# A graph layer on one core: the gather of node rows goes to GpSimd alone, and the edge product takes two tiles at once

## What is computed

```python
msg  = relu(x[src] + edge_attr @ We + be)
aggr = segment_sum(msg, dst, num_segments=N)
h    = (1.0 + eps) * x + aggr
h    = relu(h @ W1 + b1) @ W2 + b2
h    = relu((h - mean(h)) * rsqrt(var(h) + 1e-5) * gamma + beta) + x      # over the nodes
out  = layernorm(x + h)                                                   # over the features
```

## Time and profile before

| | us |
|---|---|
| device time, median of 3 | 1582.13 |
| device time, lowest and highest | 1579.88, 1583.58 |
| span of the profiled execution | 2684.1 |
| that execution's own time | not given; the page has the span alone |
| PE busy in the span (23395 matmuls) | 1871.5 |
| POOL busy (1179 gathers among 1193 instructions) | 1154.5 |
| DVE busy | 991.5 |
| ACT busy | 841.5 |

### The profile page before, as it was taken

One profiled execution on the slowest core, in us unless ns is written; L12 is line 12 of the kernel. 1 busy time (PEld: TensorE's weight loads), 2 busy tenths in 40 slices (PEclk: granted clock), 3 DMA queues, 4 the chain that ended last, 5 costly groups with the idle time before them and its releaser, 6 DMA issues.

```text
span 2684.1 us, 58837 instructions
## 1 busy us (share of the span) xinstructions
PE 1871.5 (70%) x23395; PEld 1369.8 (51%) x23395; DVE 991.5 (37%) x3361; ACT 841.5 (31%) x1954; POOL 1154.5 (43%) x1193
## 2 busy tenths in 40 slices
PE   1776777776777777677767767767767776766776
PEld 0455555555555555555555555555555555555554
DVE  6433333333333333333333333333333333333335
ACT  3232323232332333232323323323223322322335
POOL 6444444444444444444444444434434444444421
PEclk9877788787887787788888778878778778887888
DMA  8222222232222222222222222222222222222221
GB/s 231 62 59 65 62 59 68 59 71 66 63 63 61 61 62 64 61 66 59 67 61 61 65 61 63 65 58 65 64 58 67 61 62 63 63 65 62 62 86 50
DMA packets 148455, 180.61 MB, mean 67 GB/s; under 512 B 41677, under 2 KB 128932, under 8 KB 147924
## 3 DMA queue, kind: packets, MB, share of 16 engines
q1 hardware_dynamic: 102489, 89.62, 14.0%
q0 software_dynamic: 37728, 77.31, 11.5%
q10 hardware_dynamic: 7963, 9.90, 1.2%
HBM read 170.09 MB, written 6.63 MB: 66 GB/s over the span
## 4 chain that ended last, share of the span: by engine, by line
PE 66%; issue 20%; another core or an unknown queue 8%; ACT 2%; DVE 1%; ACTq 0%; DVEq 0%
PE ps L1330 23%; PE ps L1315 15%; PE ps L1255 12%; PE ps L1269 11%; PE ps L1296 1%; PE ps L1276 1%; PE ps L1299 1%; ACT xg L694 1%; PE ps L1287 1%; PE ps L1384 1%; ACT slotS L680 0%; PE ps L1288 0%; PE ps L1394 0%; DVE lnst L1197 0%
## 5 line engine op out<-in xcount | busy, mean ns | idle before, releaser
L574 POOL DMA_INDIRECT xg<-xb,idxb x1145 | 1106.6, 966 | 1423.9 <-DVE msg L937 1068.8
L1330 PE MATMUL ps<-iota_all 128*128 128x128 bf16 x4032 | 377.8, 247 | 425.7 <-issue 291.3
L688 ACT ACTIVATE iota_all<-ps 128x384 bf16<-128x384 f32 x896 | 408.5, 489 | 775.6 <-remote 567.8
L1330 PEld LDWEIGHTS ps<-iota_all 128*128 128x128 bf16 x4032 | 290.1, 111 | 515.6 <-issue 511.5
L1022 DVE TENSOR_TENSOR accT<-accT,ps 128x64 f32 x390 | 86.5, 222 | 1138.4 <-remote 992.8
L1255 PE MATMUL ps<-we,ea 64*128 64x128 f32 x3126 | 344.2, 367 | 45.7 <-issue 45.3
L1330 PE MATMUL ps<-iota_all,hot_all 128*128 128x128 bf16 x4032 | 301.1, 229 | 102.6 <-issue 98.8
L937 DVE TENSOR_TENSOR msg<-ps,xg 128x512 f32<-128x512 f32 x390 | 262.0, 686 | 238.9 <-PE ps L1255 233.2
L1330 PEld LDWEIGHTS ps<-iota_all,hot_all 128*128 128x128 bf16 x4032 | 247.2, 102 | 172.4 <-issue 145.0
L1255 PEld LDWEIGHTS ps<-we,ea 64*128 64x128 f32 x3126 | 288.0, 261 | 80.7 <-issue 72.2
L1269 PE MATMUL ps<-msg,hot 128*64 128x128 f32 x3120 | 300.9, 352 | 6.2 <-issue 4.5
(11 more groups left out here) (135 smaller groups left out, 1113.8 us busy)
## 6 DMA issues: line engine op xcount, KB each, us to landing
ea<-in_eat SPq DMA_DIRECT2D x156, 320.0 KB
lowB<-lowD SPq DMA_DIRECT2D x128, 224.0 KB
xg<-xb,idxb POOLq DMA_INDIRECT x1145
accT<-in_xt ACTq DMA_DIRECT2D x1, 3125.0 KB
x<-in_xt ACTq DMA_DIRECT2D x1, 3125.0 KB
iota_all<-in_x ACTq DMA_DIRECT2D x1, 3080.0 KB
out<-iota_all SPq DMA_DIRECT2D x5, 512.0 KB
xb<-iota_all SPq DMA_DIRECT2D x3, 784.0 KB, 6.2
```

What stands on the lines that cost most here:

```text
L574: pool.indirect_dma_start(out=xg[0:rows, slot, j, :], out_offset=None, in_=of, in_offset=bass.IndirectOffsetOnAxis(ap=index, axis=0)).then ...
L688: act.activation(rows3[:, t, :, :].rearrange("p a h -> p (a h)"), ps_rows(k * NTILE + t), ACT.Copy)\
L1330: last = pe.matmul(found[:, e, :], sel2[set_of(k)][:, t, e * P:(e + 1) * P], rows3[:, t, a, :], start=(t == 0 and e == 0 and a == 0), stop ...
```

## The change

The new kernel has nothing of TensorE's share. `x3`, the sets, the sorting, the picks and the joins are gone, and with them the lists that SP sent to HBM and back. All 1563 tiles are gathered by GpSimd, one indirect DMA for each as before, and the ring still has 15 places. The indices of all groups come in three loads at the start rather than in 78 loads along the way.

`linear` takes two tiles at once. The weights are the 128 rows of `ea` (64 features of one tile above 64 of another), and the moving operand is `we2`, 256 columns with We on the diagonal blocks and zero elsewhere; one matmul gives two tiles side by side. `place(j)` puts a group's tiles in the matching order. `msg` and `hot` have four sets instead of three; the window sums, the turned sums and `winS` have two; the edge product has two banks for each half. VectorE writes the one-hot of a pair ahead of its additions and adds a window three pairs late (`LAG`). The turned `x` that the end needs has a place of its own (`xT`) and is loaded once. The early chunks start in the last 12 pairs, one a pair.

```diff
-    RING = ROUND // 2
-    TURN = 3
+    RING = 15
+    TURN = 4
+        def place(j):
+            return (0, 2, 1, 3)[j]
+        def ps_two(m, half, c):
+            return ps[:, m % 2 * 2 + half, 2 * c * HID:2 * (c + 1) * HID]
...
-                    for j in range(by_pool(i, g)):
-                        gather(g % RING, j, P, idxb[h][:, at + j:at + j + 1], s_xg[g % RING], xb if biased else x)
+                if g == UNBIASED:
+                    for q in range(NQ):
+                        pool.wait_ge(s_xb[q], stores(q))
+                if g >= RING:
+                    wait_apart(pool, s_pre, g - RING + 1)
+                for j in range(GROUP):
+                    gather(g % RING, place(j), P, idx_all[:, h, at + j:at + j + 1], s_xg[g % RING],
+                           x if g < UNBIASED else xb)
...
-            def linear(h, s, half, tiles):
-                for j, r in tiles:
-                    rows, at = slice(j // 2 * EDIM, (j // 2 + 1) * EDIM), j % 2 * P
-                    last = pe.matmul(ps_lin(half, j)[0:r, :], ea[h][rows, s, at:at + r], we2[rows, :], start=True, stop=True)
+            def linear(m, half):
+                h, s = divmod(2 * m + half, SPAN)
+                if s == 0:
+                    pe.wait_ge(s_ea[h % PARTS], (h // PARTS + 1) * 32)
+                for c in range(2):
+                    last = pe.matmul(ps_two(m, half, c), ea[h % PARTS][:, s, c * P:(c + 1) * P],
+                                     we2[:, :, :].rearrange("k c h -> k (c h)"), start=True, stop=True)
                 last.then_inc(s_lin, 1)
...
+            for p in range(PAIRS):
+                one_hot(p)
+                add_x(p, 0)
+                add_x(p, 1)
+                if p >= LAG:
+                    add_window(p - LAG)
...
+            for p in range(PAIRS):
+                if p >= 2:
+                    pe.wait_ge(s_pre, 2 * (p - 1))
+                for half in range(2):
+                    linear(p, half)
+                if p >= 2:
+                    window(p - 2)
+                if p >= LAG:
+                    turn(p - LAG)
```

More of the change, by code:

```diff
@@ L130, in gine_layer_kernel @@
     BY_ACT = 4
-    assert BATCHES[-1][0] + BATCHES[-1][1] == NBLK and N < FAR and NSUB * SUB - N < SUB
-    BANK = BANKW
+    assert BATCHES[-1][0] + BATCHES[-1][1] == NBLK
+    FLAGS = 8
+    LAG = 3
+    CLOSE = PAIRS - EARLY
+    DONE = [2 * (CLOSE + c - LAG) for c in range(EARLY)]
+    BANK = 512
     WALL = -(-N // BANK)
@@ L1258, in _ @@
-            ALL = [(j, P) for j in (0, 2, 1, 3)]
-            def window(q, pair):
-                pe.wait_ge(s_msg, 2 * pair + 2)
-                pe.wait_ge(s_hot, pair + 1)
-                if not isinstance(pair, int) or pair:
-                    pe.wait_ge(s_winS, pair)
-                    pe.wait_ge(s_acc, 2 * pair)
-                for j in range(GROUP):
-                    for half in range(2):
-                        last = pe.matmul(ps_win[half * WIN:(half + 1) * WIN, :], hot[:, q % TURN, half * GROUP + j, :],
-                                         msg[:, q % TURN, half * GROUP + j, :], start=(j == 0), stop=(j == GROUP - 1))
-                last.then_inc(s_win, 1)
@@ new lines, in linear_last @@
+            def linear_last(m):
+                h, s = divmod(2 * m, SPAN)
+                pe.wait_ge(s_ea[h % PARTS], (h // PARTS + 1) * 32)
+                for j, r in LAST:
+                    c, at = j // 2, j % 2 * P
+                    rows = slice(c * EDIM, (c + 1) * EDIM)
+                    last = pe.matmul(ps_lin(m, 0, j)[0:r, :], ea[h % PARTS][rows, s, at:at + r], we2[rows, c, :],
+                                     start=True, stop=True)
+                last.then_inc(s_lin, 1)
@@ new lines, in window @@
+            def window(m):
+                pe.wait_ge(s_msg, 2 * m + 2)
+                pe.wait_ge(s_hot, m + 1)
+                if m >= 2:
+                    pe.wait_ge(s_winS, m - 1)
+                    pe.wait_ge(s_acc, 2 * (m - 1))
+                if m < PAIRS:
+                    for j in range(GROUP):
+                        for half in range(2):
+                            last = pe.matmul(ps_win(m)[half * WIN:(half + 1) * WIN, :], hot[:, m % TURN, half * GROUP + j, :],
+                                             msg[:, m % TURN, half * GROUP + place(j), :],
+                                             start=(j == 0), stop=(j == GROUP - 1))
+                else:
+                    for j, r in LAST:
+                        last = pe.matmul(ps_win(m)[0:WIN, :], hot[0:r, m % TURN, j, :], msg[0:r, m % TURN, place(j), :],
+                                         start=(j == 0), stop=(j == LASTT))
+                last.then_inc(s_win, 1)
@@ L1410, in _ @@
-            run(pe, iteration)
-            general, redo = held
-            pe.wait_ge(s_ea[0], (ITERS * (SPANS // PARTS) + 1) * 32)
-            pe.wait_ge(s_pre, LASTG)
-            linear(0, 0, 0, LAST)
-            window(STEPS - 1, LOOPED // 2 - 1)
-            turn(LOOPED // 2 - 1)
-            pe.wait_ge(s_msg, LASTG + 2)
-            pe.wait_ge(s_hot, LASTG // 2 + 1)
-            for m, (j, r) in enumerate(LAST):
-                last = pe.matmul(ps_end, msg[0:r, LASTG // 2 % TURN, j, :], hot[0:r, LASTG // 2 % TURN, j, :],
-                                 start=(m == 0), stop=(m == len(LAST) - 1))
```

905 lines of the change are left out of this document (217 added, 688 removed).

## The result

The changed kernel takes **2062.39 us** (2057.66 to 2065.16), the kernel before 1582.34 us beside it. The ratio is 1.3026, with a 95% interval of 1.2998 to 1.3053: 30% slower, 24 us above the 2038 us of the forecast and inside its range of 1985 to 2100. The profiled execution took 2065.16 us, 2.2 us more than its span.

What follows compares the result with a forecast made beforehand. GpSimd's issue of gathers was taken as the bound. Start 3.5, gathers 1950.6, lifts 4.3, `xb` wait 2, one-hots 36 and end 41.2 sum to 2038 us, 29% slower; range 1985 to 2100 us.

Steps and rivals of the forecast that it cites:

- GpSimd is the bound before, and its step is 1.248 us: Kernel before: GpSimd issues gathers nearly without a pause, one every 1.248 us, 1179 of them making 1471.4 us.
- The term of 1950.6 us: Main loop after the change: 1563 gathers on GpSimd at 1.248 us each.
- The reason given for the long profile: Profile before: its 2684.1 us span against 1582 timed was taken as the price of recording TensorE's instructions.
- 57 us left, within 2 to 4% of the bound: Kernel before: steps and ends sum to 1525 us, leaving 57 of 1582, of which contention takes some 24.
- TensorE stays under GpSimd's 9.98 us a pair: New loop: TensorE needs 6.5 us a pair, with up to 4.2 for the edge product, against GpSimd's 9.98.
- The rival that TensorE binds at 2385 us: New loop: single matmuls really run one behind another, 11.8 us a pair, so TensorE sets the time; chance 3%.
- The shared wait at the start: Early part: gathers held under the four lifts lose 4.3 us, which stay after the change.
- The wait for `xb`: After the first 40 gathers: GpSimd's old wait of 8.7 us becomes 0 to 10 us, taken as 2.
- The one-hots, 36 us: Loop: one-hots falling at random meet a gather's start in 54% of pairs, holding it 0.34 us; 0 to 133 us.
- The rival that saw the tie and let every one-hot meet at the full 0.68 us (2135 us): Loop: one-hots follow landings at a fixed distance, so all meet gathers, costing 133 us; over 2100 us, chance 8%.
- The end, 41.2 us: Last gather to end: 37.0 us from the last product, plus landing, additions, clips, last window's 0.9; 39 to 54.
- Nothing for what lies around the span: Outside the profiled span: what a run has around it wasn't given, so nothing was added.

Runs made afterwards that it cites:

- e3_fewer: The changed kernel with 1188 of its 1563 gathers, some tiles in every third group from group 15 on left out: 1594.80 us.
- b_again: The kernel before, unchanged, run once more for a second profiled execution: 1586.59 us.
- e5_before_less: The kernel before with two of four gathers left out, from the second round on, in each group that is GpSimd's alone; TensorE's work unchanged: 1479.31 us.
- e1_iota_psum: The changed kernel with one operand of the one-hot moved from SBUF to PSUM, except in the last 12 pairs: 2014.88 us.
- e9_before_scalar: The kernel before with the one-hot of a pair made by eight scalar-compare instructions in place of one with two SBUF operands: 1569.43 us.

## Why the prediction was right, step by step

- **GpSimd is the bound before, and its step is 1.248 us.** Right. The step was read from a profile that showed another bottleneck, and it held: 1.248 before, 1.251 after, 1.247 by `e3_fewer`. The term of 1950.6 us came out at 1955.3.
- **The reason given for the long profile was wrong.** The earlier trace rows were read as the price of recording TensorE's instructions. `b_again` has all of them and spans 1584.5 us; `e5_before_less` has 58353 and spans 1477.7 us in an execution of 1479.52. The choice to lean on the distance between gathers was good, the reason for it wasn't: that the step held is in part luck, since nobody knew what had disturbed that execution. Another execution, not an argument, settled it.
- **"57 us left, within 2 to 4% of the bound".** Too cautious. In `b_again` the sum is 3.4 until the first gather, 1471.4 of steps, 7.6 for `xb`, 5.4 lost in the first 31 gathers (34.7 busy against 31 x 0.944), 45.9 in the 1145 behind them (1126.8 against 1145 x 0.944), and 47.2 from the last gather's end to the end: 1580.9 of 1584.5 us. The contention I had at 20 us was 45.9, and the end I had at 41 was 47.2.
- **TensorE stays under GpSimd's 9.98 us a pair.** Right. Two edge products took 2.24 and 3.43 us where up to 4.2 was allowed, and the longest of all 3.8; with 1.98 for the window and 0.48 for the turn the dearest pair has 6.2 us, where 6.5 was reckoned. The rival that TensorE binds at 2385 us is out.
- **The shared wait at the start.** 4.3 us kept, measured 4.0 (41.9 busy for 40 gathers against 40 x 0.947). The wait for `xb` was put at 2 us between 0 and 10, and was 3.9. The cause is the one that the prediction feared, the load of all indices ahead of the stores on SP's queue:

```profile
7.65 35.75 SPq L299 DMA_DIRECT2D idx_last<-in_src_col  x3
...
43.44 8.24 SPq L305 DMA_DIRECT2D xb<-iota_all  x4
```

  SP gets through these loads only at 43.4 us, and the first store of `xb` goes out at 43.44 us, though its lift was done at 32; in `b_again` it goes out at 36.94, as soon as its lift is done. The first gather from `xb` starts at 61.23 us and there at 54.92. The first gather of all started at 3.56 us, after 1.9 us of waiting for its own indices.
- **The one-hots, 36 us.** The right mechanism, mis-sized: 50.3 us, 0.26 us a pair where 0.185 was worked out. The step that failed is "if it falls at random". Starts spread evenly would meet 54% of the one-hots and be held for 0.34 us each. In the trace 151 of 190 are met, 79%, most of them within 0.25 us of their start, and 50.3/151 is 0.33 us each. VectorE's pair follows the landing of a gather, and the landing follows GpSimd's steps, which ties the one to the other. In 106 of 188 pairs the one-hot starts 3.5 to 3.8 us behind the start of the last gather of the pair before, and three steps are 3.75 us. The 0.34 us for each is right by luck. A gather that starts later than 0.03 us into the one-hot is held until 0.82 us behind its end (the 0.87 read from the earlier trace rows is 0.82 there too: 1016.21 less 1015.39). That is 0.13 us less than its own 0.947, so it loses 0.56 us less its start, and not what is left of the one-hot. Evenly spread starts would then cost some 0.11 us a pair, 22 us in all (an estimate from these rows); 36 was too much for the case described, and too little for the one that came. The rival that saw the tie and let every one-hot meet at the full 0.68 us (2135 us) had its reason right and its size too large: the truth lies between the two. This term is the larger half of the 24 us missing.
- **The end, 41.2 us.** Measured 45.3, from 2017.73 to 2063.0 us. The step that was too small is the 0.9 us for the last window's copy and turn. From the last group's product to the next product (W1), after the change and in `b_again`:

```profile
2022.45 1.70 PE L844 MATMUL ps<-msg,hot 128*64 128x128 f32 x6 [0.85 <-DVE accT L644]
...
2026.90 1.81 PE L857 MATMUL ps<-accT,w1s 128*128 128x220 f32 x4 [1.90 <-issue]
```

```profile
1547.43 1.15 PE L1420 MATMUL ps<-hot,msg 128*128 128x64 f32 x6 [0.17 <-ACT msg L769]
...
1548.99 1.84 PE L1384 MATMUL ps<-accT,w1s 128*128 128x220 f32 x4 [0.41 <-DVE accT L1115]
```

  It is 4.45 us where it was 1.56: the windows are added late now, and the last ones are copied, turned and added in a row before W1. In front of it, the product waits for the addition of an earlier window, so that it starts 4.7 us behind the last gather's end and not 3.3 (the 2 for the landing, the additions and the clips). From the product on, the 37.0 us of the earlier trace rows were good: they are 37.1 in `b_again`, and 40.6 after the change. That `b_again` has 47.2 us from its last gather all the same is because its last group's product starts 10.1 us behind that gather; there the work of the loop runs on longer.
- **Nothing for what lies around the span.** It was 2.2 us.

With the measured terms: 3.6 + 1955.3 + 4.0 + 3.9 + 50.3 + 45.3 + 2.2 = 2064.6, beside the 2065.16 us of that execution. The mechanism was right; of the terms, the one-hots, the end, the wait for `xb`, the step and the time around the span all came out a little larger than reckoned.

## What to carry to other kernels

Count the instructions of the engine that issues the indirect gathers, and take its step from one start to the next: here 1.25 us a piece with 128 rows and 1.2 with 64, so a gather by matrix products on a TensorE that has room may be the cheaper half. Where a profile's span is far from the timed executions, take it again before explaining it. And when GpSimd binds, look at the longer VectorE instructions that run beside it: moving one operand to PSUM freed the gathers, and so did eight short instructions in place of one, which gave the kernel before 0.8% for an edit of a few lines, though they take VectorE twice as long.

## What the runs showed of the hardware that was not expected

- A gather is held if it starts while one of certain VectorE instructions runs; it then ends 0.81 to 0.84 us behind that instruction (1.45 us at 1001.15). The fp32 one-hot with two SBUF operands does it, and so do 16-bit `tensor_scalar` with one SBUF tensor and a column (1.08 us at 203.72 in `e9_before_scalar`). The same one-hot with one operand in PSUM doesn't: 139 gathers started in one in `e1_iota_psum` before its last 12 pairs, and none took over 0.95 us. So the engines don't meet at semaphores alone.
- One that is under way already isn't held (0.95 us at 1011.66), and one that starts within 0.03 us behind the start of the one-hot holds the one-hot by some 0.05 us instead (0.73 us at 1475.32), nine times in the loop. Eight short instructions, 1.39 us in a row, hold almost none (mean 944 ns).
- Halving the rows of a gather takes 5% off its busy time on GpSimd (0.947 to 0.900 us) and nothing off the pause behind it. From issue to landing it was 2.5 us with 128 rows and 2.3 with 64.
- TensorE's granted clock, 0.98 over the loop of the kernel before, averages 0.70 after and 0.55 with the one-tile form, between its two levels of 1.2 and 2.4 GHz. The engine idles 1016.6 us for VectorE's additions after the change. With a pause of several microseconds in every pair this costs nothing.
